# Cross-attention with a feed-forward layer on one Trainium2 core: the weight folds issued in pairs, lower and upper 64 partitions alternating

## Chip, cores and metric

The kernel runs on one core of one Trainium2 chip. The metric is the device time of one execution in microseconds (us); lower is better.

## What is computed

The reference, cut to what matters here (float32, 8 batches of 56 tokens, 1500 context rows, width 128, 16 heads of 64):

```python
def xattn(x, context, mask, Wq, Wkv, Wout, bout):
    k, v = jnp.split(context @ Wkv, 2, axis=-1)
    q = x @ Wq                                    # (8, 56, 16*64), split into heads
    dots = einsum('bhnd,bhmd->bhnm', q, k) * 64 ** -0.5
    dots = dots - (1.0 - mask)[:, None, :, None] * 1e6
    attn = softmax(dots)
    return merge_heads(einsum('bhnm,bhmd->bhnd', attn, v)) @ Wout + bout

x = x + xattn(layernorm(x), ctx_1024, mask, Wq, Wkv, Wout, bout)
x = x + ffn(layernorm(x), w1, b1, w2, b2)         # per batch: gelu(x @ w1 + b1) @ w2 + b2
```

## The kernel before

The kernel never forms k and v. For each head it multiplies two weight matrices first: w_qk[h] = Wq[h] Wk[h]^T and w_vo[h] = Wv[h] Wout[h], both 128 x 128. These products are the folds. Each contracts over the 64 elements of a head, so it uses 64 of TensorE's 128 rows. The weights lie in pairs of heads: head 2j in partitions 0 to 63, head 2j + 1 in partitions 64 to 127 of slot j (wqk_raw, an alias of ex, and wvo_raw, an alias of att_n). Fold n takes four slots, 4(n // 2) to 4(n // 2) + 3, and one half, r = n % 2, and writes one bank of 128 x 512 floats. There are four folds for w_qk and four for w_vo. Every fp32 product is issued as two LDWEIGHTS and two MATMUL instructions, so a fold has eight of each (line 344, in the helper fold).

The start. TensorE runs 20 warming instructions (keep_clock), then folds 0 and 1 of w_qk into the two banks of ps_a. ScalarE copies each to w_qk (drain_fold, line 689). TensorE transposes the first normalised tokens (line 519), forms the first queries from w_qk (line 364, into ps_s), transposes the other tokens, and then does fold 2, a maximum, fold 3, two maxima, the other first queries, and a row of maxima (line 432) alternating with later queries (line 371). A maximum is a product qk·ctxt of one 128 x 500 piece, which VectorE reduces (line 765); its result sets the shift of the softmax. VectorE works negpen (line 964) off ahead of the first reduction. Queries 2 wait for fold_drained to reach 4.

The batches. For each batch, TM = 12 steps. In step t TensorE does scores(t) (six products: qk_hi·ctxt_hi, qk_lo·ctxt_hi, then a place for jobs, then qk_hi·ctxt_lo; line 396), a place for jobs, and probs_ctx(t - 2), which is two products of ex and ctx_sb (line 424) with a place for jobs between them. The three places are (t, 0), (t, 1), (t, 2), and lists at the head of the kernel say what goes where: MAX_AT has the maxima of the next batch, (2, 2), (3, 2), (4, 0) and (4, 2) among them, and FOLD_AT has the four w_vo folds in batch 0. All such jobs use the two banks of ps_x in turn:

```python
def job():
    wait(pe, job_free, jobs.value(jobs.n - 1))
    bank = jobs.n % 2
    jobs.add()
    return ps_x[:, bank, :]
```

A job thus waits until all jobs but the latest are drained. VectorE drains them in the same order: at each place it copies a fold (folded, line 871) or reduces a maximum (line 765), and add_tile (line 762) stands between the places (t, 0) and (t, 1). When all folds are drained, GpSimd clears att_n, two steps after the last place of FOLD_AT.

Of the kernel before, what the change touches and what calls it, by code (L numbers as in the profile page):

```python
# [43 lines left out]
P = 128  # L44
# [50 lines left out]
def wait(eng, sem, value):  # L95

    if not isinstance(value, int) or value > 0:
        eng.wait_ge(sem, value)


def xattn_ffn(nc, x_pairs, ctx, ctx_t, mask_q, wq_t, wk_t, wv_t, w_out, b_out, w1, b1_t, w2, b2, out):
    B, N, D = out.shape
    M = ctx.shape[1]
    E, _, FF = w1.shape
# [32 lines left out]

    SUM_AT, Y_AT, ZT_AT, HID_AT, OUT_AT = (3, 0), (5, 2), (7, 2), (8, 1), (11, 2)
    SUM_DRAINED = (3, 2)
    FOLD_AT = [(3, 0), (3, 1), (3, 2), (4, 0)]  # L140
    SHIFT_AT = (0, 1)
    SEEDED = TM - 2
    BEHIND = 2
# [5 lines left out]
    with ExitStack() as stack:  # L149
# [3 lines left out]
        def sem(name):  # L153
            return stack.enter_context(nc.semaphore(name))
# [22 lines left out]
        wqk_raw = ex[:, :, :].rearrange("p r q -> p (r q)")[:, 0:2 * HP * P].rearrange("p (w j d) -> p w j d", w=2, j=HP)  # L177
        wvo_raw = att_n[:, :, :].rearrange("p (w j) d -> p w j d", w=2)
# [35 lines left out]
        ps_a = stack.enter_context(nc.psum_tensor("ps_a", [P, 2, 512], F32))  # L214
# [4 lines left out]
        wqk_in = [sem("wqk_in_first_half"), sem("wqk_in_second_half")]  # L219
# [4 lines left out]
        fold_filled, fold_drained = sem("fold_filled"), sem("fold_drained")  # L224
# [10 lines left out]
        job_ready, job_free = sem("job_ready"), sem("job_free")  # L235
# [94 lines left out]
        def _(pe):  # L330
            jobs = new_jobs()
# [5 lines that stand above are left out]
                jobs.add()  # L337
                return ps_x[:, bank, :]

            def fold(bank, raw, n):  # L340

                j0, r = 4 * (n // 2), n % 2
                for j in range(j0, j0 + 4):
                    mm = nc.tensor.matmul(bank[:, (j - j0) * P:(j - j0 + 1) * P],  # L344
                                          raw[64 * r:64 * r + 64, 0, j, :], raw[64 * r:64 * r + 64, 1, j, :],
                                          start=True, stop=True)
                return mm

            def fold_qk(n):

                wait(pe, fold_drained, n - 1)
                pe.wait_ge(wqk_in[n // 2], 32)
                fold(ps_a[:, n % 2, :], wqk_raw, n).then_inc(fold_filled, 1)

            def fold_vo_job(n):
                bank = job()
                if n == 0:
                    pe.wait_ge(wvo_in, 32)
                fold(bank, wvo_raw, n).then_inc(job_ready, 1)

            def queries(bank, j):

# [44 lines left out]
            def shift_rows(dst, rows, c, start):  # L407

                diag = shift_diag[:, :, :].rearrange("p t q -> p (t q)")
                return nc.tensor.matmul(dst, ones_r[:, 0:rows], diag[:, c * CH:(c + 1) * CH], start=start, stop=True)  # L410
# [73 lines left out]
            def iteration(b, prepare=True, pair=None):  # L484
                def jobs_at(at):
                    if at == SHIFT_AT:
                        for c in range(2):
                            shift_rows(job()[:, 0:CH], P, c, start=True).then_inc(job_ready, 1)
                    if b.off == 0 and at in FOLD_AT:
                        fold_vo_job(FOLD_AT.index(at))  # L490
                    if b.off > 0 and at == SUM_AT:
                        sum_jobs(b.later(-1))
                    if prepare and at in MAX_AT[b.parity]:
                        k, t = divmod(MAX_AT[b.parity].index(at), QT)
                        if t == 0:
                            pe.wait_ge(ctxt_hi_ready, b.later(1).at(KM, k + 1))
                        if (k, t) == (0, 0):
                            pe.wait_ge(qk_hi_ready, b.later(1).at(1, 0))
                        max_job(b.later(1), k, t)
                    if pair is not None:  # L500
                        for place, do in ((Y_AT, y_job), (ZT_AT, zt_job), (HID_AT, hidden_job), (OUT_AT, out_job)):
                            if at == place:
                                do(pair)

                for t in range(TM):
                    scores(b, t, lambda: jobs_at((t, 0)))
                    jobs_at((t, 1))
                    if t >= 2:
                        probs_ctx(b, t - 2, lambda: jobs_at((t, 2)))
                    elif b.off > 0:  # L510
                        probs_ctx(b.later(-1), TM - 2 + t, lambda: jobs_at((t, 2)))
                    else:
                        jobs_at((t, 2))
# [17 lines left out]
            pe.wait_ge(vec_step, 1)  # L531
            keep_clock(10)
            fold_qk(0)
            fold_qk(1)
            pe.wait_ge(ident_ready, 1)
            xnt_job(0, 1, 1)
            pe.wait_ge(job_free, jobs.value())
# [2 lines left out]
            def next_max():  # L540
                nonlocal maxima
                t, k = divmod(maxima, KM)
                pe.wait_ge(qk_drained, -(-(t + 1) * P // (4 * N)))
                pe.wait_ge(ctxt_hi_ready, k + 1)
                max_job(first, k, t)
                maxima += 1
# [7 lines left out]
            first_queries(1)  # L554
            xnt_job(1, PAIRS, 2)
            xnt_jobs = jobs.value()
            for n in (2, 3):
                fold_qk(n)
                next_max()
            next_max()  # L560
            for j in (2, 3):
                first_queries(j)
                next_max()
# [174 lines left out]
        def _(dve):  # L738
# [131 lines left out]
            def folded(n):  # L870
                nc.vector.tensor_copy(folded_heads(w_vo, n), filled().rearrange("p (j d) -> p j d", d=P)).then_inc(job_free, 1)
# [5 lines left out]
            def iteration(b, prepare=True, pair=None):  # L877
                def drain(at):
                    if at == SHIFT_AT:
                        wait(dve, seeded, b.at(SEEDED, 0))  # L880
                        for c in range(2):
                            nc.vector.tensor_copy(shift_row[:, c * CH:(c + 1) * CH], filled()[:, 0:CH]).then_inc(job_free, 1)  # L882
                    if b.off == 0 and at in FOLD_AT:
                        folded(FOLD_AT.index(at))
                    if b.off > 0 and at == SUM_DRAINED:
                        for c in range(2):
                            drain_sum(b.later(-1), c)
                    if prepare and at in MAX_AT[b.parity]:
                        max_part(*divmod(MAX_AT[b.parity].index(at), QT))
                    if pair is not None:  # L890
                        if at == Y_AT:
                            residual(pair)
                        if at == ZT_AT:
                            z_transposed(pair)
                        if at == HID_AT:
                            hidden(pair)
                        if at == OUT_AT:
                            output(pair)

                def between(at):  # L900
                    if prepare and at == QK_HI_AT:
                        qk_hi_part(b.later(1))
                    if prepare and at in CTXT_HI_AT:
                        ctxt_hi_chunk(b.later(1), CTXT_HI_AT.index(at))
                    if b.off > 0 and at == REFINE_AT:
                        refine_inverse()
                    if b.off > 0 and at == ATT_N_AT:
                        normalise_att(b.later(-1))
                    if pair is not None and at == Z_AT:
                        normalise(pair)  # L910
                    if pair is not None and at == (HID_AT[0] + 2, 1):
                        gelu_cap(pair)
                    if pair is not None and at == (HID_AT[0] + 3, 1):
                        gelu(pair)
                    if prepare and at == (TM - 1, 1):
                        shifts(b.later(1))

                for t in range(TM):
                    drain((t, 0))
                    between((t, 0))  # L920
                    if t > 1:
                        add_tile(b, t - 1)
                    elif t == 0 and b.off > 0:
                        add_tile(b.later(-1), TM - 1)
                    between((t, 1))
                    drain((t, 1))
                    between((t, 2))
                    drain((t, 2))
                    between((t, 3))
# [70 lines left out]
        def _(pool):  # L1000
# [15 lines left out]
            def iteration(b, prepare=True):  # L1016
                for t in range(TM):
                    if b.off == 0 and t == FOLD_AT[-1][0] + 2:

                        pool.wait_ge(job_free, FIRST_JOBS - sum(at > FOLD_AT[-1] for at in MAX_AT[0]))  # L1020
                        nc.gpsimd.memset(att_n[:, :, :], 0.0).then_inc(att_n_ready, 1)
# [78 lines left out]
```

## Time and profile before

| | |
|---|---|
| median of 3 runs | 408.41 us (407.51 to 409.65) |
| profiled execution | 407.78 us, span of the trace 406.0 us |
| TensorE matmul / weight load busy | 394.8 us (97%) / 285.1 us (70%) |
| VectorE, ScalarE, GpSimd busy | 302.7, 206.1, 57.6 us |
| granted TensorE clock | 0.999 over the span |

The span is the time between the first and the last instruction of the trace. Times in the trace count from its start. PE is TensorE's matmul stream, PEld its weight loads, DVE VectorE, ACT ScalarE, POOL GpSimd, SP the queue that issues DMAs. A MATMUL's record lasts longer than the step to the next one, since they are pipelined.

### The profile page before, as it was taken

The page shows a single profiled execution, that of the slowest core. Times are in us where ns is not written, and L with a number is a line of the kernel's source. Part 1 is how long each engine was busy: PE and PEld are TensorE (multiplying, and loading weights), DVE is VectorE, ACT ScalarE, POOL GpSimd, SP SyncE. Part 2 cuts the span into 40 slices and gives each one's busy share as a digit, 9 for nine tenths or more (in the row PEclk, how much of TensorE's full clock was granted, in tenths as well). Part 3 has the DMA queues.
Part 4 walks back from the last instruction along what each step waited for, and adds up shares of the span by engine and source line. Part 5 has one row for each costly group of instructions (what it writes and reads, how often), then busy time and mean ns, then how long its engine had stood idle before and what let it go on. Part 6 is the DMA issues. An engine that isn't in the chain of part 4 may idle for free.

```text
span 406.0 us, 5555 instructions
## 1 busy us (share of the span) xinstructions
PE 394.8 (97%) x1721; PEld 285.1 (70%) x1721; DVE 302.7 (75%) x490; ACT 206.1 (51%) x274; POOL 57.6 (14%) x47
## 2 busy tenths in 40 slices
PE   8998999999999999999999999999999999999995
PEld 7765777766776876767676877667776776676684
DVE  4889578878797689877887689877887687365443
ACT  3546354466437445565556444665366444755431
POOL 0603040600060000600060001500060000000000
PEclk9999999999999999999999999999999999999999
DMA  7660020050005000043005000161011001200000
GB/s 252 206 200 19 2 76 1 2 147 5 2 0 141 12 2 2 13 127 120 0 7 144 0 0 0 35 173 53 0 30 45 0 0 39 70 2 0 3 2 3
DMA packets 20661, 19.62 MB, mean 48 GB/s; under 512 B 904, under 2 KB 17576, under 8 KB 20648
## 3 DMA queue, kind: packets, MB, share of 16 engines
q1 hardware_dynamic: 20648, 19.45, 15.5%
q8 instruction: 8, 0.13, 0.1%
q14 instruction: 5, 0.04, 0.0%
HBM read 19.21 MB, written 0.23 MB: 48 GB/s over the span
## 4 chain that ended last, share of the span: by engine, by line
PE 93%; DVE 4%; ACT 2%; issue 1%; ACTq 0%
PE ps_a L424 35%; PE ps_s L396 28%; PE ps_x L432 10%; PE ps_x L451 4%; PE ps_x L439 3%; PE ps_a L371 2%; PE ps_s L526 2%; PE ps_x L471 2%; PE ps_x L480 2%; PE ps_s L410 2%; PE ps_x L344 1%; PE ps_s L364 1%; DVE log_sum L793 1%; PE ps_a L344 1%; ACT inv_sum L635 1%
## 5 line engine op out<-in xcount | busy, mean ns | idle before, releaser
L424 PE MATMUL ps_a<-ex,ctx_sb 125*128 125x448 f32 x384 | 172.2, 541 | 0.0
L605 ACT ACTIVATE ex<-ps_s 125x896 f32<-125x896 f32 x96 | 88.0, 917 | 118.9 <-PE ps_s L396 92.8
L765 DVE TENSOR_REDUCE chunk_max<-ps_x 128x1 f32<-128x500 f32 x168 | 111.2, 673 | 31.9 <-PE ps_x L432 28.9
L432 PE MATMUL ps_x<-ctxt_hi,qk_hi 128*128 128x500 f32 x168 | 88.6, 530 | 4.9 <-DVE log_sum L793 3.6
L424 PEld LDWEIGHTS ps_a<-ex,ctx_sb 125*128 125x128 f32 x384 | 71.3, 189 | 27.6 <-issue 21.6
L762 DVE TENSOR_TENSOR ex_sum<-ex_sum,ex 125x896 f32<-125x896 f32 x80 | 86.5, 1081 | 4.6 <-ACT ex L605 4.6
L396 PE MATMUL ps_s<-qk_hi,ctxt_hi 128*125 128x448 f32 x192 | 87.1, 535 | 0.0
L612 ACT COPY ps_s<-shift_row 125x896 f32<-125x896 f32 x80 | 72.9, 911 | 9.9 <-DVE shift_row L882 7.8
L396 PEld LDWEIGHTS ps_s<-qk_hi,ctxt_hi 128*125 128x125 f32 x192 | 35.8, 187 | 35.5 <-issue 35.1
L396 PE MATMUL ps_s<-qk_hi,ctxt_lo 128*125 128x448 f32 x192 | 57.2, 379 | 0.0
L396 PE MATMUL ps_s<-qk_lo,ctxt_hi 128*125 128x448 f32 x192 | 54.7, 366 | 0.0
L1007 POOL TENSOR_TENSOR qk_lo<-qk,qk_hi 128x448 fp32r<-128x448 f32 x16 | 23.7, 1483 | 217.5 <-DVE qk_hi L786 216.0
L432 PEld LDWEIGHTS ps_x<-ctxt_hi,qk_hi 128*128 128x128 f32 x168 | 31.5, 188 | 24.8 <-issue 8.1
L396 PEld LDWEIGHTS ps_s<-qk_hi,ctxt_lo 128*125 128x125 f32 x192 | 35.6, 186 | 6.8 <-issue 2.6
L396 PEld LDWEIGHTS ps_s<-qk_lo,ctxt_hi 128*125 128x125 f32 x192 | 35.6, 185 | 3.3
L1013 POOL TENSOR_TENSOR ctxt_lo<-ctxt_raw,ctxt_hi 128x500 fp32r<-128x500 f32 x24 | 32.0, 1348 | 11.3 <-DVE ctxt_hi L782 11.3
L782 DVE CAST ctxt_hi<-ctxt_raw 128x500 fp32r<-128x500 f32 x24 | 23.7, 1019 | 0.0
L793 DVE TENSOR_TENSOR log_sum<-ps_x,inv_sum 128x448 f32<-128x448 f32 x16 | 9.3, 619 | 18.6 <-ACT inv_sum L635 18.6
L451 PEld LDWEIGHTS ps_x<-w_vo,att_n 128*128 128x128 f32 (+1 forms) x160 | 18.1, 170 | 1.5 <-issue 1.2
L451 PE MATMUL ps_x<-w_vo,att_n 128*128 128x128 f32 (+1 forms) x160 | 18.6, 275 | 0.0
L629 ACT ACTIVATE log_sum<-ps_x 128x448 f32<-128x448 f32 x16 | 8.7, 542 | 10.7 <-PE ps_x L439 10.6
L648 ACT ACTIVATE logv<-veps 128x1 f32<-128x1 f32 (+2 forms) x7 | 1.4, 203 | 24.7 <-DVE veps L828 22.5
(79 smaller groups left out, 272.4 us busy)
## 6 DMA issues: line engine op xcount, KB each, us to landing
ctxt_raw<-in_ctx_t SPq DMA_DIRECT2D x8, 750.0 KB, 7.3
ctx_sb<-in_ctx SPq DMA_DIRECT2D x8, 750.0 KB
w_sb<-in_w SPq DMA_DIRECT2D x4, 512.0 KB, 3.7
w_sb<-in_w SPq DMA_DIRECT2D x8, 256.0 KB, 4.3
ex<-in_wq_t SPq DMA_DIRECT2D x2, 256.0 KB, 3.8
ex<-in_wk_t SPq DMA_DIRECT2D x2, 256.0 KB, 4.6
att_n<-in_wv_t SPq DMA_DIRECT2D x1, 512.0 KB, 6.0
att_n<-in_w_out SPq DMA_DIRECT2D x1, 512.0 KB, 6.8
```

What stands on the lines that cost most here:

```text
L396: mm = nc.tensor.matmul(dst[c], a[:, u, rows], q[:, u, chunks[c]], start=(n == 0 and not seed), stop=(n == 2 and seed), skip_group_check=seed)
L424: mm = nc.tensor.matmul(ps_a[:, c, 0:CH], ctx_sb[0:MT, u, t, :], ex[0:MT, t % RING, c * CH:(c + 1) * CH], start=(t == 0), stop=(t == TM - 1))
L432: nc.tensor.matmul(bank[:, 0:MC], qk_hi[:, u, t * P:(t + 1) * P], ctxt_hi[:, u, k * MC:(k + 1) * MC], start=True, stop=True).then_inc(job_ ...
L451: mm = nc.tensor.matmul(bank[pair.tokens(), 0:D], att_n[:, h, pair.tokens()], w_vo[:, h, :], start=(h == 0), stop=(h == HEADS - 1))
L605: nc.scalar.activation(half(ex[0:MT, slot, :]), src, ACT.Exp, scale=SCALE).then_inc(ex_ready, 1)
L612: nc.scalar.copy(ps_s[0:MT, t % 2, :, 0:CH], half(shift_row[0:MT, :])).then_inc(seeded, 1)
L762: nc.vector.tensor_tensor(dst, left, ex[0:MT, t % RING, :], ALU.add).then_inc(ex_summed, 1)
L765: nc.vector.tensor_reduce(chunk_max[:, k, t:t + 1], filled()[:, 0:MC], AX.X, ALU.max).then_inc(job_free, 1)
L782: nc.vector.tensor_copy(ctxt_hi[:, b.parity, k * MC:(k + 1) * MC], ctxt_raw[:, k * MC:(k + 1) * MC]).then_inc(ctxt_hi_ready, 1)
L793: nc.vector.tensor_tensor(log_sum[:, cols], bank[:, 0:CH], inv_sum[:, cols], ALU.mult).then_inc(job_free, 1)
L1007: nc.gpsimd.tensor_tensor(qk_lo[:, b.parity, cols], b.pick(qk)[:, cols], qk_hi[:, b.parity, cols].bitcast(F32), ALU.subtract).then_inc(qk_ ...
L1013: nc.gpsimd.tensor_tensor(ctxt_lo[:, b.parity, cols], ctxt_raw[:, cols], ctxt_hi[:, b.parity, cols].bitcast(F32), ALU.subtract).then_inc(c ...
```

## The change

Folds n = 2m and n = 2m + 1 are issued as one pair. Their products alternate, one from partitions 0 to 63 into one bank, one from partitions 64 to 127 into the other. Each half's last product raises the semaphore. The w_qk pairs go to the two banks of ps_a. The w_vo pairs take two jobs at once; FOLD_AT has two places instead of four. In the start, the maximum that stood between folds 2 and 3 stands behind the pair. The copies are the same eight.

```diff
-    FOLD_AT = [(3, 0), (3, 1), (3, 2), (4, 0)]
+    FOLD_AT = [(3, 0), (3, 2)]
...
-            def fold(bank, raw, n):
-                j0, r = 4 * (n // 2), n % 2
-                for j in range(j0, j0 + 4):
-                    mm = nc.tensor.matmul(bank[:, (j - j0) * P:(j - j0 + 1) * P],
-                                          raw[64 * r:64 * r + 64, 0, j, :], raw[64 * r:64 * r + 64, 1, j, :],
-                                          start=True, stop=True)
-                return mm
-            def fold_qk(n):
-                wait(pe, fold_drained, n - 1)
-                pe.wait_ge(wqk_in[n // 2], 32)
-                fold(ps_a[:, n % 2, :], wqk_raw, n).then_inc(fold_filled, 1)
-            def fold_vo_job(n):
-                bank = job()
-                if n == 0:
+            def fold_pair(banks, raw, m, filled):
+                for j in range(4):
+                    cols = slice(j * P, (j + 1) * P)
+                    for r, bank in enumerate(banks):
+                        rows = slice(64 * r, 64 * r + 64)
+                        mm = nc.tensor.matmul(bank[:, cols], raw[rows, 0, 4 * m + j, :], raw[rows, 1, 4 * m + j, :],
+                                              start=True, stop=True)
+                        if j == 3:
+                            mm.then_inc(filled, 1)
+            def fold_qk(m):
+                wait(pe, fold_drained, 2 * m)
+                pe.wait_ge(wqk_in[m], 32)
+                fold_pair([ps_a[:, 0, :], ps_a[:, 1, :]], wqk_raw, m, fold_filled)
+            def fold_vo_jobs(m):
+                banks = [job(), job()]
+                if m == 0:
                     pe.wait_ge(wvo_in, 32)
-                fold(bank, wvo_raw, n).then_inc(job_ready, 1)
+                fold_pair(banks, wvo_raw, m, job_ready)
...
                     if b.off == 0 and at in FOLD_AT:
-                        fold_vo_job(FOLD_AT.index(at))
+                        fold_vo_jobs(FOLD_AT.index(at))
...
             fold_qk(0)
-            fold_qk(1)
...
-            for n in (2, 3):
-                fold_qk(n)
+            fold_qk(1)
+            for _ in range(3):
                 next_max()
-            next_max()
...
                     if b.off == 0 and at in FOLD_AT:
-                        folded(FOLD_AT.index(at))
+                        for r in range(2):
+                            folded(2 * FOLD_AT.index(at) + r)
```

## Rows read from the trace of the kernel before

**Rows 1.** The page: TensorE's busy time, and the chain that ended last, by engine.
```profile
PE 394.8 (97%) x1721; PEld 285.1 (70%) x1721; DVE 302.7 (75%) x490; ACT 206.1 (51%) x274; POOL 57.6 (14%) x47
...
PE 93%; DVE 4%; ACT 2%; issue 1%; ACTq 0%
```
**Rows 2.** PE in flight at 6.72 and 11.30 us; line 344's durations (min/median/max).
```profile
6.38 0.60 PE L344 MATMUL ps_a<-ex 64*128 64x128 f32 x6
...
11.04 0.50 PE L344 MATMUL ps_a<-ex 64*128 64x128 f32 x3
...
L344 PE MATMUL ps_a<-ex x32: 272/272/579, 5.6 to 13.1; 64*128 64x128 f32 x32
...
L344 PE MATMUL ps_x<-att_n x32: 272/272/373, 40.5 to 48.2; 64*128 64x128 f32 x32
```
**Rows 3.** Timeline of 0 to 17 us: start, duration, engine, line, operation.
```profile
5.63 1.92 PE L344 MATMUL ps_a<-ex 64*128 64x128 f32 x16
...
7.02 1.14 ACT L689 COPY w_qk<-ps_a 128x512 f32<-128x512 f32 x2 [2.40 <-PE ps_a L344]
...
8.28 1.86 PEld L364 LDWEIGHTS ps_s<-inv_sum,w_qk 128*128 128x128 f32 x16 [0.67 <-DVE inv_sum L874]
...
10.72 1.16 PE L344 MATMUL ps_a<-ex 64*128 64x128 f32 x8
...
11.80 0.49 PE L432 MATMUL ps_x<-ctxt_hi,qk_hi 128*128 128x500 f32 x1
11.91 0.59 ACT L689 COPY w_qk<-ps_a 128x512 f32<-128x512 f32 x1 [0.78 <-PE ps_a L344]
...
12.41 0.68 DVE L765 TENSOR_REDUCE chunk_max<-ps_x 128x1 f32<-128x500 f32 x1
...
13.41 0.59 ACT L689 COPY w_qk<-ps_a 128x512 f32<-128x512 f32 x1 [0.92 <-PE ps_a L344]
...
14.06 1.15 PE L364 MATMUL ps_s<-inv_sum,w_qk 128*128 128x112 f32 x8
```
**Rows 4.** The chain of 0 to 60 us in order: start, us, work.
```profile
33.69 2.53 DVE ctxt_hi L782 x2
...
36.82 0.04 issue
...
41.64 0.60 PE ps_s L396 x2
...
45.79 0.75 PE ps_a L424 x2
46.54 0.81 PE ps_s L396 x4
47.35 1.09 PE ps_x L344 x8
48.44 0.42 PE ps_x L432
48.86 0.40 PE ps_s L396 x2
...
50.01 0.23 PE ps_x L432
```
**Rows 5.** Timeline of 36 to 52 us: TensorE's first w_vo fold and VectorE's queue.
```profile
39.00 1.25 DVE L765 TENSOR_REDUCE chunk_max<-ps_x 128x1 f32<-128x500 f32 x2
...
40.48 1.16 PE L344 MATMUL ps_x<-att_n 64*128 64x128 f32 x8
...
41.67 0.69 DVE L871 COPY w_vo<-ps_x 128x512 f32<-128x512 f32 x1 [1.42 <-PE ps_x L344]
...
42.28 1.08 DVE L762 TENSOR_TENSOR ex_sum<-ex_sum,ex 125x896 f32<-125x896 f32 x1
```
**Rows 6.** The load of ctxt_raw for batch 1: issue and landing.
```profile
L274 SPq DMA_DIRECT2D ctxt_raw<-in_ctx_t x1: 709/709/709, 18.5 to 18.5; - x1
...
DMA to landing us min/median/max: 7.7/7.7/7.7
```

## The prediction

> **What bounds the kernel now.** I read the page first: TensorE (PE) is busy for 97% of the span and holds 93% of the chain that ended last [rows 1]. So a change to the folds, which are TensorE work, counts only as far as it shortens TensorE's own path and does not put waits into it. The folds are 32 fp32 products in all; each shows as two MATMULs and two LDWEIGHTS. 16 products make w_qk before the first queries, 16 make w_vo inside the first batch.
>
> Next I read the start and the stretch of the w_vo folds in order of time and as a chain [rows 3 to 5]. One fold, four products from the same half, holds TensorE for 1.09 us in the chain [rows 4]. Half of the array idles meanwhile: a product uses 64 rows.
>
> The row that decides the matter is already in the kernel before. Folds 0 and 1 are issued without a wait between them, one from partitions 0 to 63, the other from 64 to 127. At 6.72 us six MATMULs of line 344 are in flight, where a fold by itself has three [rows 2]. The 16 MATMULs took 1.92 us; one fold took 1.16, a second behind it at a step of 0.11 per MATMUL ((1.16 - 0.27 - 0.11)/7) would make 2.05, and the slow start adds 0.21 (the longest MATMUL of these folds, the very first, lasted 0.579, the longest of the w_vo folds 0.373 [rows 2]). 2.26 - 1.92 = 0.34, or three steps, were saved [rows 3]. So the second half's stream runs beside the first's at an unchanged step; it started late only because all of fold 0 was queued ahead of it. In the new order the other half's product is never more than one product away.
>
> **The change, part by part.**
>
> *A pair of folds.* The work is the same 16 MATMULs, in two streams of eight. I take the pair at the length of one fold, 1.09 us. Bounds: 1.09 if the streams overlap wholly, 1.09 + 8 x 0.11 = 1.98 if not at all.
>
> *Entering and leaving.* Behind a fold the next work pays for the change from 64 to 128 rows: two products that else take 0.40 took 0.60, a maximum that takes 0.23 took 0.42 [rows 4]. The entry lies inside the 1.09. Each fold taken out of the path therefore gives 1.09 + 0.19 = 1.28.
>
> *w_vo.* Two of four folds leave the path: 2 x 1.28 = 2.57 gained. But a pair takes both banks of ps_x, and this adds waits on VectorE (DVE). I lay the queue out from [rows 4, 5]:
> - Pair A starts at 40.48 as fold 0 did; the reductions of the maxima before it (two, 1.25 from 39.00) end at 40.25, so its second bank is free in time. TensorE leaves it 1.09 later, at 41.57. VectorE copies bank one from 41.67 and, 0.61 later (copies and what follows start that far apart), bank two from 42.28 to 42.97. The add of 1.08 that stood at 42.28 is now third in VectorE's queue.
> - TensorE: the two scores products with exit cost 0.60, the first half of ex·ctx 0.75, the entry 0.1: ready at 42.90. Pair B needs both copies: 42.97 + 0.04 (what a VectorE result takes to restart TensorE, [rows 4]) = 43.01. Wait 0.11.
> - Pair B ends at 44.10. Its first copy runs 44.20 to 44.89 (the add is done at 43.97). The maximum that stands behind pair B at (3, 2) needs that bank: 44.93. Wait 0.83. Before, this maximum found a free bank. Queued behind it on TensorE are the second half of ex·ctx and the scores of step 4, which go as late as it does.
> - The next job, the maximum at (4, 0), comes 0.33 + 0.75 + 0.81 later (0.33 is a maximum's 0.23 and 0.1 for weights that could not be loaded ahead, half of the exit's 0.19; the others are in rows 4), at 46.8; the second copy is done at 45.50. No wait.
> Net 2.57 - 0.94 = 1.63 us. From there each engine has the queue it had. GpSimd's clearing of att_n moves forward with the folds and lies on no path.
>
> *w_qk, second pair.* Before: fold 2 at 10.72, a maximum, fold 3, two maxima, queries at 14.06, when ScalarE's (ACT's) second copy, from 13.41, is done [rows 3]. After: the pair ends at 11.80, the copies take 1.14 from 11.91 (as the two at 7.02 did) and end at 13.05, so they no longer decide. Three maxima now stand before the queries with two banks; the third waits for the first reduction, which cannot start before 12.41 (VectorE is at negpen until then) and ends at 13.09. With 0.1 to restart and 0.33 until the next product can start, queries begin at 13.5. Gain 0.55.
>
> *w_qk, first pair.* TensorE is free 0.4 us sooner, but queries wait for ScalarE's two copies, 7.02 + 1.14 = 8.16, then start at 8.28. Fold 0's last product keeps its time, since fold 0 already ran at full step, and fold 1's is done before ScalarE reaches it. Gain 0; the bound is a loss of 0.11, if fold 0 slips a step.
>
> *Does the 0.55 last?* Behind the queries TensorE and VectorE feed each other up to the first scores. The one clocked thing is the load of the next batch's ctxt_raw: issued at 18.5, landed 7.7 later, at 26.2; the casts that need it stand on the chain from 33.69 [rows 4, 6], the first of them a little before. It keeps a slack of 5 us and more.
>
> Sum: 1.63 + 0.55 = 2.2 us. The profiled execution took 407.78 us around a span of 406.0, so it would take 405.6; the median of the runs shown is 408.41, 0.6 above it, and my time is 408.41 - 2.2 = 406.2.
>
> **The rivals.**
>
> *Partial overlap.* If the look ahead that held the second stream back in fold 0 and 1 still holds it back (three steps of eight saved), a pair takes 1.09 + 5 x 0.11 = 1.65. That costs 0.56 at each w_vo pair, about 0.5 at the second w_qk pair (the copies end at 13.6) and 0.45 at the first, whose first copy starts later: 2.2 - 2.1 = 0.1, 408.3. Against it: the other half's first product is now behind two MATMULs, not eight.
>
> *No overlap: the other side.* The place is the pair itself. Serial, each is 0.89 longer; at w_vo that turns 1.63 into -0.15; at the second w_qk pair the first reduction moves to 13.2 and queries to 14.3, -0.27; at the first, fold 0's last product comes six steps later, 0.67, and ScalarE's copies with it. Sum -1.1: 409.5, slower. It decides from the point where a pair takes more than about 1.7 us (2.2 spread over four pairs, the early ones counting a little less). Rows 2 speak against it. If, worse, each change between the halves cost 0.39 as one fold's entry and exit do, 28 changes more would add 11 us: 420. Folds 0 and 1 show no gap where they meet [rows 2].
>
> *The waits for the banks take it back.* My sum has 0.94 of them. If the second copy of pair A had to stand behind the 1.08 add, pair B would wait that much longer and the gain would be 1.1: 407.3. The order of the queue speaks against it: both copies stand before the add. The Trainium skill, TensorEngine Tiling (Array Packing), Performance Considerations, says the same of any such packing: the array gets faster, the evacuation of PSUM does not and may become the limit. By that rule, taken as the whole story, w_vo would give nothing, and 408.41 - 0.55 = 407.9 would be left. The trace agrees as far as the two waits of 0.94 go; against the rest of it stand copies 0.61 apart beside 1.09 of products [rows 5]. To the waits as the limit, by either working, I give 0.08.
>
> *More than forecast.* No wait at (3, 2) worth naming, and queries 2 bound by ScalarE's copies alone (13.05 + 0.1, so 0.9 before 14.06): up to 2.57 + 0.9 = 3.5, 404.9.
>
> **How the numbers follow.** Forecast (gain 1.7 to 2.7) 0.62; partial overlap 0.10; waits 0.08; no overlap 0.07; more 0.10; a cost at each change of half 0.03. The time is the likeliest case's, 406.2. The range takes in the bounds of the waits, partial overlap, the best case, and the spread of the runs shown (407.51 to 409.65): 404.9 to 408.3. 0.5% is 2.04 us, about what a measurement of this kernel can tell from no change, and my gain of 2.2 lies just past it: of the forecast's 0.62 I give 0.40 to faster, with the 0.10 of the better case 0.50. The rest of it, partial overlap and no overlap (0.27%) are within 0.5%: 0.46. Slower 0.04.
>
> **What would show it right or wrong.** Line 344's successor: at a moment inside a w_vo pair five or six MATMULs in flight; pair from first LDWEIGHTS to the next foreign one 1.1 us, not 1.6 or 2.0. VectorE's two w_vo copies back to back, 0.61 apart, and the add behind them. TensorE idle about 0.1 before pair B and 0.8 before the maximum behind it, ended by VectorE's copy. Queries 2 at 13.5; queries 0 still at 8.3. From the second batch on, the same queue, 2.2 us earlier. Wrong would be: a pair near 2 us, gaps between the halves, a longer MATMUL step than 0.11, or a stretch later on that swallows the lead (a DMA, or VectorE in the first batch).

## The result

| | before | after |
|---|---|---|
| median | 408.12 us (22 runs) | 405.94 us (22 runs, 405.18 to 408.42) |
| span of the profiled execution | 406.0 us | 403.9 us |
| ratio | 1 | 0.9951, 95% interval 0.9937 to 0.9964 |

The change takes 2.2 us off, as forecast (406.2 us was forecast against 405.94 measured; the difference is the base, 408.41 from three runs and 408.12 from 22). The interval lies below 1. Its middle, 0.49%, lies just short of the 0.5% that was named as what can be told from no change; the forecast, 0.54%, lay just past it.

Executions whose mean granted TensorE clock is below 0.998 mostly take about 2 us longer, and a median "at full clock" leaves them out: it is 405.75 for the changed kernel (17 of 22) and 408.07, 408.12 and 407.97 for the kernel before in the three sets of experiments.

**The profile after.** The chain that ended last, from 36 us on, stands beside [rows 4] (line 346 is 344 of before, 426 is 424, 434 is 432, 398 is 396):

```profile
36.23 0.04 issue
36.28 0.50 PE ps_x L434
...
39.96 1.09 PE ps_x L346 x16
41.05 0.60 PE ps_s L398 x2
41.65 0.75 PE ps_a L426 x2
42.41 0.11 issue
42.52 1.18 PE ps_x L346 x16
43.70 0.68 DVE w_vo L871
44.38 0.04 issue
44.43 0.49 PE ps_x L434
44.92 0.75 PE ps_a L426 x2
45.67 0.81 PE ps_s L398 x4
...
46.71 0.41 PE ps_s L398 x2
```

Sixteen MATMULs take the 1.09 us that eight took in [rows 4] (1.18 in pair B, which starts after a wait). The two waits are in it: 0.11 us before pair B, and behind pair B the chain passes through VectorE's copy instead of going straight on. The restart at 36.23 stood at 36.82 before, so the start gave 0.59 us. The work of the last row, at 46.71, stood at 48.86 before. It is 2.15 us earlier, so the w_vo folds gave 1.56.

VectorE's queue in the same stretch, by time, against [rows 5]:

```profile
41.08 1.29 DVE L871 COPY w_vo<-ps_x 128x512 f32<-128x512 f32 x2 [1.42 <-PE ps_x L346]
...
42.29 1.08 DVE L762 TENSOR_TENSOR ex_sum<-ex_sum,ex 125x896 f32<-125x896 f32 x1
42.49 1.00 PEld L346 LDWEIGHTS ps_x<-att_n 64*128 64x128 f32 x16 [0.81 <-DVE w_vo L871]
...
44.43 0.49 PE L434 MATMUL ps_x<-ctxt_hi,qk_hi 128*128 128x500 f32 x1 [0.75 <-DVE w_vo L871]
```

Two copies back to back, the add behind them, and TensorE idle for 0.75 us until the first of pair B's copies is done. The start, by time, against [rows 3]:

```profile
5.91 1.16 PE L346 MATMUL ps_a<-ex 64*128 64x128 f32 x16 [0.77 <-DMA ex<-in_wk_t]
...
7.10 1.07 ACT L689 COPY w_qk<-ps_a 128x512 f32<-128x512 f32 x2 [2.48 <-PE ps_a L346]
...
8.32 2.01 PE L366 MATMUL ps_s<-inv_sum,w_qk 128*128 128x112 f32 x16 [0.99 <-ACT w_qk L689]
...
10.73 1.16 PE L346 MATMUL ps_a<-ex 64*128 64x128 f32 x16
...
11.93 1.07 ACT L689 COPY w_qk<-ps_a 128x512 f32<-128x512 f32 x2 [0.78 <-PE ps_a L346]
12.44 2.01 DVE L765 TENSOR_REDUCE chunk_max<-ps_x 128x1 f32<-128x500 f32 x3
...
13.26 0.47 PE L434 MATMUL ps_x<-ctxt_hi,qk_hi 128*128 128x500 f32 x1 [0.71 <-DVE chunk_max L765]
...
13.57 1.04 PE L366 MATMUL ps_s<-inv_sum,w_qk 128*128 128x112 f32 x8
```

The first queries start at the old time, though the weights landed 0.3 us later in this execution: the first MATMULs, slow in [rows 3], ran at the full step here (why is told in the last section). The second queries start at 13.57 instead of 14.06; what they wait for is the third maximum, and that one waits for VectorE.

### The profile page after: what moved, and what is told of

It is laid out like the page before. It is cut to its first block, busy times and chain, and to the rows that moved or that the text cites. A ratio compares the mean times of both kernels' runs of the same rounds, so it can differ in the third digit from the quotient of the medians.

```text
span 403.9 us, 5555 instructions
## 1 busy us (share of the span) xinstructions
PE 390.0 (97%) x1721; PEld 281.2 (70%) x1721; DVE 302.8 (75%) x490; ACT 206.0 (51%) x274; POOL 57.6 (14%) x47
## 4 chain that ended last, share of the span: by engine, by line
PE 90%; DVE 5%; ACT 2%; issue 1%; DMA 1%; SPq 0%; ACTq 0%; DVEq 0%
PE ps_a L426 35%; PE ps_s L398 28%; PE ps_x L434 10%; PE ps_x L453 4%; PE ps_x L441 3%; PE ps_a L373 2%; PE ps_x L473 2%; PE ps_x L482 2%; PE ps_s L412 2%; DMA ex<-in_wk_t 1%; DVE log_sum L793 1%; DVE ctxt_hi L782 1%; ACT inv_sum L635 1%; PE ps_s L528 1%; PE ps_x L412 1%
```

## The experiments

The step of the argument that carries most is that the two halves of the array work side by side. The rivals to it are the queue's order and the two banks. Eleven runs were made: on these rivals, on the two parts of the change, and on the waits. Each diff is against the changed kernel.

**Same half, two banks.**

```diff
-                    for r, bank in enumerate(banks):
-                        rows = slice(64 * r, 64 * r + 64)
+                    for g, bank in enumerate(banks):          # w_vo pairs; r is 0 in the first, 1 in the second
+                        rows = slice(64 * r, 64 * r + 64)
...
-                            folded(2 * FOLD_AT.index(at) + r)
+                            folded(2 * r + FOLD_AT.index(at))
```

> The changed kernel, but a w_vo pair takes two folds of the same half: products still alternate between the two banks of ps_x, but all from partitions 0 to 63 in the first pair and from 64 to 127 in the second. Theory (what overlaps is the two halves of the array's rows): nothing overlaps, a w_vo pair takes 1.09 + 0.89 = 1.98 us, and of the gain only the w_qk part is left, 0.4 us below the kernel before, ratio 0.999. Rival (writing to two banks in turn is what lets the products overlap): 1.1 us a pair, 2.1 us below before, ratio 0.995.

Measured: 407.69 us at full clock (5 of 12 runs; 409.27 over all, ratio 1.002, 1.0003 to 1.0036), 0.4 below before at full clock, the total that the theory gave. The w_vo pairs by time:

```profile
40.13 2.05 PE L357 MATMUL ps_x<-att_n 64*128 64x128 f32 x16
...
43.46 2.05 PE L357 MATMUL ps_x<-att_n 64*128 64x128 f32 x16
```

The changed kernel's pair takes 1.16 from its first MATMUL's start to its last one's end, as one fold did [rows 5]; this one 2.05, eight steps of 0.11 more. In the middle of the changed kernel's pair, at 40.48 us, six MATMULs are in flight (first start, time to the last end):

```profile
40.22 0.50 PE L346 MATMUL ps_x<-att_n 64*128 64x128 f32 x6
```

The same-half pair has two or three in flight. The banks alternate in both. So it is the halves that overlap, and writing to two banks gives nothing by itself. That the total came out so close is partly luck. In the chain this kernel loses 1.40 us from the first pair to the scores of step 4 (7.11 against 5.71), not the 1.78 of the theory: the wait before pair B is gone, and pair B's last MATMULs run beside VectorE's first copy. The first queries of this execution start at 8.57, 0.25 later than in the changed kernel, for the reason told in the last section.

**The halves in turn, and two by two.**

```diff
-                for j in range(4):
-                    for r, bank in enumerate(banks):
+                for r, bank in enumerate(banks):
+                    for j in range(4):
```

> The changed kernel, but within each pair the four products of the lower half are issued first and then the four of the upper half; banks, waits and places stay those of the pair. Theory (a half that waits behind eight MATMULs of the other starts late, as folds 0 and 1 showed in the kernel before): three of eight steps overlap, a pair takes 1.09 + 5 x 0.11 = 1.65 us from its first weight load to the next foreign one, and nearly the whole gain is gone: 0 to 0.4 us below the kernel before, ratio 0.999 to 1.000. Rival A (TensorE finds the other half's products in its queue whatever the order): 1.1 us a pair and 2.1 us below before, ratio 0.995. Rival B (no overlap when issued in turn): 1.98 us a pair, 1.1 us above before, ratio 1.003.

Two by two, the order of (half, product) is 00 01 10 11 02 03 12 13:

```diff
-                for j in range(4):
-                    for r, bank in enumerate(banks):
+                for r, j in [(r, 2 * g + i) for g in range(2) for r in range(2) for i in range(2)]:
```

> The changed kernel, but within a pair two products of the lower half are issued, then two of the upper, then two and two: between the orders one by one and four by four. Theory (the other half is found if it stands no more than about five instructions behind): the upper half starts about one or two steps late and each half may be held up again at the middle, a pair takes 1.2 to 1.35 us, and the time is 0.2 to 0.6 us above the changed kernel, ratio to the kernel before 0.996 to 0.9965. Rival (any distance of two products is within reach): the same as the changed kernel.

In turn: 406.63 us, ratio 0.9975 (0.9957 to 0.9993); 406.61 at full clock. Two by two: 406.07 us, ratio 0.9955 (0.9934 to 0.9976); 406.05 at full clock, 0.3 above the changed kernel and inside what was expected; its trace shows less of a loss (below). First in turn, then two by two, one w_vo pair each:

```profile
43.72 1.71 PE L346 MATMUL ps_x<-att_n 64*128 64x128 f32 x16
44.92 1.29 DVE L871 COPY w_vo<-ps_x 128x512 f32<-128x512 f32 x2 [1.42 <-PE ps_x L346]
```

```profile
39.73 1.26 PE L346 MATMUL ps_x<-att_n 64*128 64x128 f32 x16
```

A pair takes 1.16 one by one, 1.26 two by two, 1.71 in turn, 2.05 from one half: 0, 1, 5 and 8 steps more than a fold. That is what the theory gave for each pair. But its sum for the kernel in turn was wrong: I expected the gain to be all but gone, and 1.5 us of it stayed. The row of VectorE shows why. Its first copy starts at 44.92, 1.20 us after the pair's start, just as with alternation (41.08 against 39.89): the lower half's bank is filled at the old time and is copied while the upper half is still at work. Two by two, the chain from the first w_vo pair to the scores of step 4 takes 5.71 us (39.80 to 45.51), as in the changed kernel, and the stretch from the first queries to the last two reductions before batch 0 is 19.73, 0.07 more than there. So the trace has 0.1 us of loss, not the 0.3 of the medians.

**In turn for one kind of pair only.** This was made to find out where the delay in turn is paid. The edit is the same, for w_vo or for w_qk alone.

> The changed kernel with the products of the w_vo pairs issued in turn (four of the lower half, then four of the upper); w_qk pairs alternate. Theory from the in-turn run: a pair takes 1.64 instead of 1.09 us, but its lower bank is filled at the old time, so VectorE's first copy runs beside the upper half's products; the second pair then starts 0.45 us later than with alternation, and the maximum behind it, which waits for that first copy alone, loses nothing more. 0.45 us above the changed kernel, ratio to before 0.996. Rival (each pair costs its whole 0.56): 1.1 us above.

> The changed kernel with the products of the w_qk pairs issued in turn; w_vo pairs alternate. Theory: the first pair costs nothing, since ScalarE's first copy starts as early as before; the second pair ends at 12.4 instead of 11.8, the first maximum is reduced 0.45 us later (12.9 instead of 12.44), the third maximum and queries 2 with it: 0.45 us above the changed kernel, ratio to before 0.996. Rival (hidden, ScalarE or VectorE covers it): the same as the changed kernel.

Measured: w_vo in turn 406.75 us, ratio 0.9962 (0.9937 to 0.9987), 406.59 at full clock; w_qk in turn 406.56 us, ratio 0.9952 (0.993 to 0.9974), also 406.56 at full clock. Both medians are 0.8 above the changed kernel's, measured in another set, which is more than the 0.45 expected, and both together gave 0.86; so the medians, from different sets, don't settle sums this small. The traces do. The chain, w_vo in turn:

```profile
40.94 1.64 PE ps_x L357 x16
42.58 0.61 PE ps_s L409 x2
43.18 0.75 PE ps_a L437 x2
43.94 1.10 PE ps_x L357 x11
45.03 0.02 issue
45.06 0.70 DVE w_vo L882
...
47.05 0.81 PE ps_s L409 x4
```

From the first pair to the scores of step 4 it takes 6.11 us, the changed kernel 5.71: 0.40 lost, where 0.55 are lost in each pair. The chain leaves pair B after its lower half (x11) and goes to VectorE's copy, so pair B's upper half is hidden. With w_qk in turn, queries 2 start at 14.12, 0.55 later than in the changed kernel, because VectorE's first reduction starts at 12.97 instead of 12.44; the first pair costs nothing (queries 0 at 8.31). The delay of 0.55 is still there at the last two reductions before batch 0 (28.52 against 27.97). The two traces add up to 0.95, beside the 0.86 of both together. The rival "its whole length each" is out, and so is "hidden".

**Each part alone.** The first run has the w_vo folds single and at their four old places, the second has the w_qk folds as before:

```diff
-    FOLD_AT = [(3, 0), (3, 2)]
+    FOLD_AT = [(3, 0), (3, 1), (3, 2), (4, 0)]
...
-                banks = [job(), job()]
+                bank = job()
```

> Only the w_qk folds are made in pairs; the w_vo folds are single and at their four old places. Theory: 0.5 to 0.6 us below the kernel before (ratio 0.9985), all of it from the second pair: queries 2 start at 13.5 and queries 0 still at 8.3. Rival (the first pair gives something as well, or the start is absorbed later by a load): 1.0 us, or 0.

```diff
-            fold_qk(1)
-            for _ in range(3):
+            for n in (2, 3):
+                fold_qk(n)
                 next_max()
+            next_max()
```

> Only the w_vo folds are made in pairs; the w_qk folds are as in the kernel before. Theory: 1.6 us below the kernel before (ratio 0.996), with TensorE waiting 0.1 us before the second pair and 0.8 us behind it. Together with the run that pairs w_qk alone it adds up to the whole change, 2.1 to 2.2. Rival (the two parts share a gain, for instance through VectorE's queue in the first batch): the parts add up to clearly more or less than 2.2.

Measured: w_qk alone 407.59 us, ratio 1.000 (0.9985 to 1.0014), 407.48 at full clock, 0.6 below before; w_vo alone 406.66 us, ratio 0.997 (0.9948 to 0.9993), 406.58 at full clock, 1.5 below. They add up to 2.1, and the whole gave 2.3 by the same kind of median. That w_qk alone is faster rests on its median at full clock and on the trace, not on its ratio: from the first queries to the last two reductions of the start it takes 19.64 us (8.11 to 27.75), the kernel before 20.25, w_vo alone 20.26. In w_vo alone the stretch from the first pair to the scores of step 4 takes 5.71 us, as in the changed kernel. So the traces split the gain as the sum did.

**The waits for banks taken away.** Pair B goes to (4, 0). The maximum of that place goes to (7, 2), in batch 0 only:

```diff
-    FOLD_AT = [(3, 0), (3, 2)]
+    FOLD_AT = [(3, 0), (4, 0)]
+    FIRST_MAX_AT = sorted([at for at in MAX_AT[0] if at != (4, 0)] + [(7, 2)])
```

> The changed kernel with its two waits for banks taken away by moving work: the second w_vo pair goes from place (3, 2) to (4, 0), and the maximum that stood at (4, 0) in batch 0 goes to the free place (7, 2), so that 1.35 us of other TensorE work stands between the second pair and the next job. Theory (the waits of 0.11 and 0.83 us are paid on the path, and nothing else takes them): both go to zero and it runs 0.9 us below the changed kernel, 3.1 below the kernel before, ratio 0.9925. Rival (VectorE is what sets the pace of the first batch, and the wait comes back at a later maximum): the same as the changed kernel, ratio 0.995.

Measured: 405.47 us, ratio 0.9933 (0.9909 to 0.9957); 405.17 at full clock (5 of 7 runs), 0.6 below the changed kernel, span 402.9 against 403.9. The chain:

```profile
39.93 1.09 PE ps_x L351 x16
41.02 0.60 PE ps_s L403 x2
41.62 0.76 PE ps_a L431 x2
42.37 0.23 PE ps_x L439
42.60 0.75 PE ps_a L431 x2
43.36 0.81 PE ps_s L403 x4
44.17 1.09 PE ps_x L351 x16
45.26 0.60 PE ps_s L403 x2
...
47.59 0.82 PE ps_s L403 x4
```

VectorE is gone from this stretch of the chain, and no wait came in its place. From pair A to the scores of step 5 it takes 7.66 us (39.93 to 47.59) against 8.90 in the changed kernel (39.96 to 48.86); 0.23 of the 1.24 is the maximum that moved, so 1.0 was the waits' (0.94 in my sum). The rival, a wait that comes back at a later maximum, is out.

**Queries sooner.** Two maxima instead of three stand between the second w_qk pair and queries 2:

```diff
-            for _ in range(3):
-                next_max()
-            for j in (2, 3):
-                first_queries(j)
-                next_max()
+            next_max(); next_max()
+            first_queries(2)
+            next_max(); next_max()
+            first_queries(3)
+            next_max()
```

> The changed kernel with one maximum moved in the start: two maxima instead of three between the second w_qk pair and queries 2, and two behind them. The third had to wait for VectorE's first reduction, which ends at 13.1 us. Theory: queries 2 start at 13.15, when ScalarE's two copies are done, and the lead of 0.4 us lasts: 0.4 below the changed kernel, ratio to the kernel before 0.994. Rival (VectorE's string of 21 reductions, begun at 12.4, is what ends last before batch 0, and it loses the time at the third reduction): the lead is gone by the time of the first shift, the same as the changed kernel.

> The changed kernel with both moves: the second w_vo pair at (4, 0) with the maximum of (4, 0) at (7, 2), and queries 2 ahead of the third maximum. Theory: the two gains add, 1.3 us below the changed kernel, 3.4 to 3.5 below the kernel before, ratio 0.9915. Rival (one of the two is taken back): 0.4 or 0.9 below the changed kernel.

> The kernel with both moves, but with one maximum, not two, between queries 2 and queries 3, and two behind queries 3. In the run with both moves, the second of two maxima in a row found its bank still with VectorE. Theory (that wait took 0.2 of the 0.4 us that earlier queries gave): up to 0.2 us below the kernel with both moves, ratio to before 0.9905. Rival (the wait comes back at the next maximum, since the reductions have to be done one after the other): the same as with both moves.

Measured: sooner alone 405.88 us, ratio 0.993 (0.9907 to 0.9954); both moves 404.8 us, ratio 0.9907 (0.9884 to 0.993); both with a later maximum (two, queries 2, one, queries 3, two) 405.2 us, ratio 0.9911 (0.9875 to 0.9946). All 18 of their runs were at full clock. To compare the start of these traces, I count again from the first queries to the last two reductions before the shift, since the first pair's own length differs from run to run (below). In the chain these are 8.31 and 28.56 in the kernel before, the 20.25 us above. In the changed kernel:

```profile
27.97 1.27 DVE chunk_max L765 x2
```

with queries at 8.31, so 19.66. Queries sooner, from 8.70:

```profile
13.43 1.15 PE ps_s L366 x8
...
15.04 0.88 PE ps_s L366 x8
15.92 0.24 PE ps_x L434
16.16 0.10 issue
16.26 0.46 PE ps_x L434
...
28.18 1.27 DVE chunk_max L767 x2
```

19.48 us, so 0.18 of the expected 0.4 lasts; at 16.16 a maximum waits for its bank, with VectorE behind on the reductions. In its median it shows no gain over the changed kernel (405.88 against 405.75). The later maximum made this worse: its chain enters VectorE's reduction for 0.69 us at 15.71, and the count is 20.01 (8.44 to 28.45). So both sides of the expectation for the sooner queries were partly right: they do start sooner, and the string of reductions takes more than half of it back. With the later maximum neither side came true: it was expected at most 0.2 us below the kernel with both moves, and it lies 0.4 above. For both moves together the rival was right: 0.95 us below the changed kernel, not 1.3. Nearly all that the kernel with both moves gains over the changed one is the waits for banks. It is the best version: 404.8 us, 3.3 below before.

## Why the prediction was right

- *A pair is as long as a fold.* Forecast 1.09 us, measured 1.09 where no wait stands before it. The rows of folds 0 and 1 [rows 2] were read rightly, and so was the reason that their overlap was only three steps: in turn, each pair has three again. The same-half run shows that it is the halves of the array.
- *Entry and exit, 1.28 us for each fold taken out.* The net of w_vo was forecast at 1.63 and measured at 1.56.
- *The two waits.* Forecast 0.11 and 0.83 us; the chain has 0.11, and TensorE idles 0.75 before the maximum, counted from the end of the last MATMUL's record. The forecast counted from the time at which the next work could have started, 1.09 after pair B's start; counted so it is 0.82 (42.52 + 1.09 to 44.43). Moving them off the path gave 1.0 for the 0.94 of the sum. The Trainium skill, TensorEngine Tiling (Array Packing), Performance Considerations, says that tiling speeds up TensorE but not the evacuation of PSUM, which may become the bottleneck. The trace agrees at these two places and in the start, where TensorE waits 0.99 us for ScalarE's copies and 0.71 for VectorE's reduction; it is not the story of the whole, for w_vo still gained 1.56.
- *Second w_qk pair.* Forecast 0.55 (queries 2 at 13.5); measured 0.49 at queries 2 (13.57) and 0.59 at the start of batch 0, since the row of queries 2 is also shorter, 1.04 us against 1.15 [rows 3].
- *First w_qk pair.* Forecast 0. Queries 0 stood still (8.28 to 8.29, by their first weight load), but that these two traces agree is luck: the weights landed 0.28 us later, and the clock was at its full level 1.7 us sooner (4.41 against 6.08 us). The forecast rests better on traces whose clock rose at nearly the same time. With the rise at 6.08 us queries 0 start at 8.31 (the kernel before), with the rise at 6.17 and alternating products at 8.28 (w_vo in turn). In w_vo alone and w_qk alone, with the rise at 5.68 and 5.83, it is 8.11 and 8.12.
- *The lead lasts.* 2.15 us at 46.7 us, 2.1 at the end of the span.
- *Of the rivals*, partial overlap is what issuing in turn gives, but my price for it was wrong. I charged 2.1 us for 0.56 per pair; the run lost 0.86. The failed step is that a longer pair delays everything behind it. Of the four terms charged, two were paid: the first w_vo pair (0.44, since its 0.55 also takes away the wait of 0.11 before pair B) and the second w_qk pair (0.55). The other two, 0.56 for pair B and 0.45 for the first w_qk pair, were not: what waits behind these waits first for the copy of the lower half's bank, and that bank is filled at the old time (TensorE is released by that copy at 45.76 in w_vo in turn, and ScalarE's first copy starts at 7.02 in w_qk in turn as in the kernel before). The lengths of the pairs themselves stand. With products of one half, where both banks are filled late, the price was nearer, 1.40 us in the chain for a forecast of 1.78, again too high because VectorE's copy begins before the pair ends.

## What to carry to other kernels

Products that contract over 64 rows (here fp32, 128 columns) can be had two for one if the other half's product stands next in the queue, one by one. Each half had a bank of its own in all these runs; whether both halves could write to one bank was not tried. A pair fills two banks at once, so look at what stands behind it: other work that needs no bank should lie there, at least as long as the copies take. Before paying for a finer order, ask which half the next consumer waits for; if it is the first one, an unequal finish costs less than it seems.

## What the runs showed of the hardware that I had not expected

How far TensorE reaches for the other half's products shows as a count: with 2, 4 and 8 MATMULs of one half issued before the other's first, the pair ended 0, 1 and 5 steps late (1.16, 1.26, 1.71 us), as if the other half starts once about three are left before it. I have no run with other counts.

The length of the first w_qk pair differs between executions of the same code, and the time at which TensorE's clock rises accounts for it. MATMULs of this pair, changed kernel, queries sooner, and in turn (min/median/max in ns):

```profile
L346 PE MATMUL ps_a<-ex x16: 272/272/373, 5.9 to 6.8; 64*128 64x128 f32 x16
...
L346 PE MATMUL ps_a<-ex x16: 271/417/580, 5.6 to 7.2; 64*128 64x128 f32 x16
...
L346 PE MATMUL ps_a<-ex x16: 417/418/578, 5.8 to 8.5; 64*128 64x128 f32 x16
```

At the start TensorE steps 0.21 us from one MATMUL to the next, twice the 0.11 of later, which fits the lower of its two levels (1.2 against 2.4 GHz). It is busy with the warming instructions from 1.06 us on in all of them. The clock's own record in each trace says when the full level begins, and the step halves there. For the pairs that alternate:

| trace | clock at full level from, us | first pair in the chain, us | queries 0 at, us |
|---|---|---|---|
| changed kernel (weights 0.28 later) | 4.41 | 1.21 | 8.32 |
| w_qk alone | 5.83 | 1.23 | 8.12 |
| w_vo in turn | 6.17 | 1.39 | 8.28 |
| no bank wait | 6.24 | 1.43 | 8.32 |
| both, later maximum | 6.49 | 1.54 | 8.44 |
| both | 6.73 | 1.65 | 8.55 |
| same half | 6.79 | 1.68 | 8.57 |
| queries sooner | 7.03 | 1.80 | 8.70 |

In the kernel before the rise is at 6.08 us, queries 0 at 8.31. In the profiled execution of the in-turn kernel it came only at 13.99 us: the first pair took 3.09 us and the first queries nearly twice their usual time:

```profile
5.83 3.09 PE ps_a L346 x16
...
9.71 3.76 PE ps_s L366 x16
```

These queries take 2.01 us in the chain of the kernel before and of the changed one. That execution took 410.0 us, where the kernel's median is 406.6, though its mean granted clock is 0.998: the mean counts the time ahead of the first clock record as full. So a late rise doesn't show in the mean, and at a kernel's start the step between MATMULs tells the clock. It moves the first queries of these traces by up to 0.6 us (8.12 to 8.70), so effects of some tenths of a us are read here from stretches that begin behind it and not from the medians. Why the rise comes at 4.4 us in one execution and at 14 in another, these runs don't show.
